# First convolution: the fourth row combination of every second unit moves from GpSimd to VectorE

## The reference

```python
x = x + _L0_conv_ref(_gn(x), ...)   # group norm, 1x1 conv to q, k, v, depthwise 3x3 conv,
                                    # attention over channels, 1x1 conv out
x = x + _L1_conv_ref(_gn(x))        # 3x3 patches, nearest channel per group, floor of products
```

```python
qkv = jax.lax.conv_general_dilated(x, w_qkv, (1, 1), 'SAME', dimension_numbers=DN) + b_qkv
qkv = jax.lax.conv_general_dilated(qkv, w_dw, (1, 1), 'SAME', dimension_numbers=DN, feature_group_count=3 * C) + b_dw
```

## Time and profile before

| what | us |
|---|---|
| median of 3 runs (lowest, highest) | 1471.12 (1470.74, 1479.9) |
| the profiled execution: its time | 1469.96 |
| its span in the profile | 1468.2 |
| first convolution, first image, about | 50 to 249 of the span |
| first convolution, second image, about | 768 to 967 of the span |

### The profile page before, as it was taken

One profiled execution on the slowest core, in us unless ns is written; L12 is line 12 of the kernel. 1 busy time (PEld: TensorE's weight loads), 2 busy tenths in 40 slices (PEclk: granted clock), 3 DMA queues, 4 the chain that ended last, 5 costly groups with the idle time before them and its releaser, 6 DMA issues. The chain is left out here.

```text
span 1468.2 us, 34011 instructions
## 1 busy us (share of the span) xinstructions
PE 1312.2 (89%) x13586; PEld 1050.8 (72%) x13586; DVE 1142.1 (78%) x1896; ACT 886.8 (60%) x1013; POOL 654.3 (45%) x672
## 2 busy tenths in 40 slices
PE   3889998996999599999979999989959968999998
PEld 1788897996899355555549998979949954555554
DVE  6577777477873699999967777745877838999998
ACT  3566664311553399999955556532135409999996
POOL 4888894242220244434038998814422113344400
PEclk9999999998999699999999999999979978999999
DMA  5466632593225344464427865319405235274533
GB/s 213 125 185 199 204 110 54 155 310 113 88 75 230 114 136 119 140 163 94 121 97 251 253 209 166 89 30 278 107 1 216 109 109 169 77 188 107 149 72 103
DMA packets 75876, 210.27 MB, mean 143 GB/s; under 512 B 15306, under 2 KB 15414, under 8 KB 72646
## 3 DMA queue, kind: packets, MB, share of 16 engines
q1 hardware_dynamic: 61214, 158.10, 34.1%
q0 software_dynamic: 6720, 36.93, 9.5%
q10 hardware_dynamic: 7784, 13.07, 3.3%
HBM read 91.54 MB, written 67.04 MB: 108 GB/s over the span
## 5 line engine op out<-in xcount | busy, mean ns | idle before, releaser
L1780 PE MATMUL acc<-rnd,ident 128*128 128x376 f32 x1152 | 391.9, 484 | 13.6 <-ACT rnd L1757 13.6
L1780 PEld LDWEIGHTS acc<-rnd,ident 128*128 128x128 f32 x1152 | 216.9, 192 | 134.0 <-ACT rnd L1757 15.0
L956 PE MATMUL ps_a<-wa,shared 128*128 128x192 f16 x1536 | 296.7, 247 | 9.3 <-DMA xc<-low 7.4
L956 PE MATMUL ps_a<-wb,xb 128*128 128x192 f16 x1536 | 295.5, 246 | 0.0
L1752 ACT ACTIVATE rnd_m<-prod,plus_round,scale 128x1504 f32<-128x1504 f32 x144 | 235.7, 1637 | 40.3 <-DVE prod L1603 30.3
L1716 DVE SCALAR_TENSOR_TENSOR over<-prod,scale,rnd 128x1504 bf16<-128x1504 f32 x144 | 256.4, 1783 | 0.0
L574 POOL TENSOR_TENSOR vt<-z 96x256 f32<-96x256 f32 x248 | 253.2, 1041 | 3.6 <-ACT z L850 3.5
L1757 ACT ACTIVATE rnd<-rnd_m,minus_round 128x1504 f32<-128x1504 f32 x144 | 223.2, 1550 | 4.7
L1660 POOL DMA_INDIRECT near<-f_planes,index x42 | 120.4, 2866 | 148.5 <-DVE prod L1603 142.4
L956 PEld LDWEIGHTS ps_a<-wa,shared 128*128 128x128 f16 x1536 | 150.6, 98 | 12.3 <-DMA xc<-low 8.5
L956 PE MATMUL ps_a<-wfa,shared 128*128 128x96 f16 x1536 | 155.7, 206 | 3.2 <-issue 2.8
(11 more groups left out here) (344 smaller groups left out, 2450.7 us busy)
## 6 DMA issues: line engine op xcount, KB each, us to landing
xb<-shared ACTq DMA_DIRECT2D x64, 195.0 KB, 2.7
f_planes<-img SPq DMA_DIRECT2D x8, 1536.0 KB, 14.1
shared<-f_planes SPq DMA_DIRECT2D x16, 768.0 KB, 5.8
v_a<-shared SPq DMA_DIRECT2D x40, 260.0 KB, 2.7
v_b<-xb SPq DMA_DIRECT2D x40, 260.0 KB, 3.1
shared<-v_a SPq DMA_DIRECT2D x40, 260.0 KB, 4.8
xb<-v_b SPq DMA_DIRECT2D x40, 260.0 KB, 5.5
v_c<-xc SPq DMA_DIRECT2D x40, 195.0 KB, 3.3
```

Source lines behind the costliest of these rows:

```text
L956: mm = lambda a, w, first, end: nc.tensor.matmul(out(i), a, w, start=first, stop=end)
L1780: nc.tensor.matmul(o(m), k["ident"][:, :], rnd[:, n % RNDS, BR * m:BR * m + BR, :], start=False, stop=False, skip_group_check=True)
```

## The change

In units 6, 8, ..., 30 (13 of 32, in each image) GpSimd leaves out combination 3; VectorE makes it, in `last_term`, at the end of its unit u-4 list, behind qk_low(2(u-4)+1). A semaphore `v_shared` counts these, and ScalarE's `high` and `norm` wait for it as well as for `v_made`.

```diff
+        SHARED = list(range(6, UNITS, 2))
+        shared_by = lambda u: sum(s <= u for s in SHARED)
...
                 for i, (p_, q_, op) in enumerate(V_TERMS):
-                    if i in which:
+                    if i in which and not (i == 3 and u in SHARED):
                         last = nc.gpsimd.tensor_tensor(out[:, i], row(p_), row(q_), op)
                 if 3 in which:
                     last.then_inc(v_made, 1)
...
+            def last_term(u):
+
+                at, out = 4 * (u % 4), vt[:, u % 2].rearrange("p (j i) x -> p i j x", i=4)
+                p_, q_, op = V_TERMS[3]
+                dve.wait_ge(normed, u + 2)
+                dve.wait_ge(lo_done, u - 1)
+                nc.vector.tensor_tensor(out[:, 3], z[:, at + p_:at + p_ + 3:2, :], z[:, at + q_:at + q_ + 3:2, :], op
+                                        ).then_inc(v_shared, 1)
...
                 qk_low(2 * u + 1)
+                if u + AHEAD + 1 in SHARED:
+                    last_term(u + AHEAD + 1)
...
                     act.wait_ge(v_made, u)
+                    act.wait_ge(v_shared, shared_by(u))
...
                     act.wait_ge(v_made, u - 3)
+                    act.wait_ge(v_shared, shared_by(u - 3))
```

More of the change, by code:

```diff
@@ L409 @@
             "outs", "o_s", "o_t", "o_a", "evac") \
-    + ("rows_ready0", "rows_ready1", "parts_in0", "parts_in1", "parts_in2", "saved0", "saved1", "saved2",
+    + ("v_shared", "rows_ready0", "rows_ready1", "parts_in0", "parts_in1", "parts_in2", "saved0", "saved1", "saved2",
        "dup_in0", "dup_in1", "dup_in2")
@@ L462, in attention @@
          att_pe, att_act, wf_split, pivot_in, pivot_out, outs, o_s, o_t, o_a, evac) = (sems[n] for n in ATT_SEMS[:34])
+        v_shared = sems["v_shared"]
+        SHARED = list(range(6, UNITS, 2))
+        shared_by = lambda u: sum(s <= u for s in SHARED)
         rows_ready = [sems[f"rows_ready{j}"] for j in range(2)]
```

## The result

The changed kernel took 1492.24 us (median of 4 runs, 1478.39 to 1498.25) against 1475.51 us (4 runs, 1470.74 to 1481.20) for the kernel before: a ratio of 1.0119, interval 1.0077 to 1.0161. The forecast was 1478.6 us with 1464 to 1485. The direction was right, the size was not: some 17 us lost instead of 7.5. The forecast started from 1471.1 us, the median of three runs of before; with the fourth run it is 1475.5, so 4.4 of the 13.6 us between 1478.6 and 1492.2 are the starting point.

What follows compares the result with a forecast made beforehand. The prediction took VectorE, ScalarE and GpSimd, not TensorE, to set the pace: 16 x 0.55 = 8.8, less 1.2, less 0.1, plus 7.5 us on 1471.1 gives 1478.6 us, range 1464 to 1485.

Steps and rivals of the forecast that it cites:

- the ring: VectorE, ScalarE and GpSimd waiting on one another in the first convolutions; said to set the pace, 6.11 or 6.21 us per unit.
- The turns: VectorE instructions with two SBUF inputs and GpSimd's never run together; when one ends, the other side's waiting instruction goes on.
- case A: At a changed boundary even_sum goes first after low; y_s at 4.32 us against a mean of 3.50, costing 0.82 us.
- case B: At a changed boundary VectorE keeps its turn behind low; y_s at 3.77 us against a mean of 3.50, costing 0.27 us.
- The second half: From y_s of a unit's first pair to y_s of its second; claimed to stay at 2.66 us.
- half A and half B: Equal mix of the two orders after low, because 24 of 55 kept the turn before: plus 0.55 us per plain boundary.
- plain boundaries: Second-pair y_s to next unit's first y_s, without transfer wait, small copies or cast: 16 places, 8.8 us lost.
- The second rival: Always even_sum first, also against last_term at the small copies: 13.1 plus 1.6, 14.7 us lost, 1485.8 us; beyond 1%: 0.07.
- the boundaries with ScalarE's small copies: First image, into units 5, 7, 11, 13, 15: GpSimd empty when low ends; gains 0.22 at four, 0.31 into 7, together 1.2 us.
- the cast: VectorE's 0.61 us instruction in the boundary into unit 3, first image: 4.32 or 3.77 against 4.13, about minus 0.1 us.
- the four places where a transfer was to hide the change: Into units 9 and 17 of each image, high waits 2.18 us for a transfer; last_term's 0.27 to 0.82 hides there, 0.
- The rival that rested on VectorE's twofold speed: VectorE keeps its turn over qk_low, last_term and td: y_s at 3.14, 7.1 us gained, 1464.0 us; chance 0.16.

Runs made afterwards that it cites:

- the first experiments: The changed kernel timed again unedited: 1488.37 us (6 runs), ratio 1.0131; the kernel before beside it took 1470.20 us (11 runs).
- in the gap: Against the changed kernel, same units: last_term moved between y_s and qk_low of the unit's first pair, where VectorE waits for ScalarE; 1462.01 us, ratio 0.9942.
- in all units and GpSimd held: last_term between the first pair's y_s and qk_low, units 4 to 30; GpSimd starts combinations 0 and 1 only after that pair's td; 1447.17 us, ratio 0.9834.

## Why the prediction was wrong

**Right.** The view that decided was the timeline of the ring, not the shares: GpSimd at 90% was relieved and the kernel became slower. The turns hold: the replay gave 4.32 for case A and 3.77 for case B, the traces show 4.31 to 4.33 and 3.78 to 3.79. The second half stayed at 2.66 us, and boundaries into even units stayed at 3.45 or 3.55, both with the few exceptions named under the table. TensorE's spare time of 0.35 us per unit was correctly taken as what is left above its 5.76.

**The step that failed** is "I take half A and half B, since before 24 of 55 kept the turn". The changed kernel took A at 15 of 16 plain boundaries. 16 x 0.55 = 8.8 us became 3.91 + 8.05 = 12.0. The share of the kernel before was no evidence for the kernel after: the change altered both lists at that point, and the outcome goes with the lists (1 of 19 with `last_term` behind `qk_low`, 15 of 19 without it). Why it does so stays open. The second rival ("always case A") was the right one at the plain boundaries (13.1 us forecast, 12.0 measured), and had too small a chance; its other half, a loss of 1.6 us at the small copies, did not come.

The sum was 9.2 us short of the 16.7 of the medians: 3.2 by this step, 1.9 by the smaller terms below, and some 4 by what the two traces do not show in the first convolutions at all.

**Terms that were a bit off.** At the boundaries with ScalarE's small copies I had `y_s` at 3.23. The timeline of after, into unit 13:

```profile
135.96 0.56 DVE L645 TENSOR_TENSOR y_s<-ps_a,td 128x384 f32<-128x384 f32 x1 [0.54 <-POOL td L585]
...
138.10 0.41 DVE L632 TENSOR_TENSOR vt<-z 96x256 f32<-96x256 f32 x1
138.24 0.99 POOL L585 TENSOR_TENSOR td<-side 128x192 f32<-128x192 f32 x1 [1.69 <-ACT side L884]
138.43 0.35 DVE L638 TENSOR_TENSOR td<-side 128x192 f32<-128x192 f32 x1
139.32 0.56 DVE L645 TENSOR_TENSOR y_s<-ps_a,td 128x384 f32<-128x384 f32 x1 [0.54 <-DVE td L638]
```

GpSimd was empty when `low` ended, as I wrote, but then `td` too went ahead of `even_sum`, which ended at 3.27, and `y_s` needs both: 3.36 us, a gain of 0.09 and not 0.22. Into unit 5 it was 3.25 and into 7 3.93, with 3.83 forecast. Together 0.66 us and not 1.2. At the cast I took nearly nothing and it cost 0.32 (4.45 for 4.13). And of the four places where a transfer was to hide the change, the two in the second image showed 0.72 us: into unit 9 the boundary and second half went from 6.95 to 7.19, into 17 from 6.79 to 7.27.

**From 12.6 to 17 us.** The trace's own sum is 3.69 + 8.91 = 12.6 us, its Gram copies say 13.5; 1.7 us more arose between the two first convolutions. The span grew by only 8.6 us, so some 5 us came back behind the second Gram copy. Instruction by instruction, ScalarE is 13.5 us late at that copy, 10.9 some 140 us later, and 8.4 at its end. The 140 us behind the copy, before and then after:

```profile
969.00:1109.00 140.00, 120.91 (x2270) 113.81 (x2268) 94.65 (x320) 40.48 (x73) 43.65 (x78) 0.93 0.40 107
```

```profile
982.50:1119.90 137.40, 118.93 (x2269) 112.31 (x2268) 94.66 (x320) 40.47 (x73) 43.69 (x78) 0.94 0.39 109
```

The same work took 2.6 us less there, at a granted clock of 0.93 and 0.94 of full speed (2.4 GHz). Another 2.2 us came back over the last 255 us, at 0.99 in both. So the clock can hold a part of it at most, and where the rest came from is open.

The medians went the other way. In the runs of the first experiments the mean granted clock over the span was 0.9609 before (11 runs) and 0.9567 after (6). Seven runs of before at 0.962 or more took 1468.9 us in the mean, the two of after at 0.963 1479.8: 10.9 more. The two of before at 0.957 or less took 1474.6 us, the four of after there 1491.4. A straight line of time against clock, through 35 of the 36 runs of before (without one of 1487.05) and through all ten of the changed kernel, gives 1470.9 and 1485.0 us at a clock of 0.960: 14.1 us apart, give or take some 3. So I estimate that a part of the 17 us, some 3 to 4, goes with a lower mean clock of TensorE in the changed kernel's runs. Whether the change lowers it or the runs fell so is open: there are too few runs for that, and no kernel here changes the clock alone.

**Moving work between the two engines.** The Trainium skill (Perfetto Trace Analysis, section Optimizing Scalar/DVE Operations) says that moving operations between GpSimd and VectorE might not help, since they share a port. The measured ratios agree with "might": 1.0131 with `last_term` behind `qk_low`, 0.9942 with it in the gap, 0.9834 with it there in all units and GpSimd held. The rival that rested on VectorE's twofold speed (0.41 against 0.72 us) did not come about in the place where the change put the instruction.

## What to carry to other kernels

When two engines take turns at a shared resource, the price of a moved instruction is not its duration: it is its own turn, and one of the other engine's turns for each gap it opens there, filled with whatever that engine has pending next. Look what stands behind the removed instruction in its engine's list before a gain is counted, and put the added one where its engine waits anyway: 0.41 us of VectorE cost 0.86 us behind `qk_low` and 0.03 in the gap. All this holds when the other engine has something pending; where it had nothing, the added instruction cost only itself (3.78 us into unit 27). A share of outcomes counted in the kernel before (24 of 55) is no chance for the kernel after, if the change touches the list at that point; both outcomes belong in the range.

## What the runs showed that I had not expected

Behind VectorE's `low`, with `qk_low` and an instruction of GpSimd both waiting, the kernel before went either way (24 to 31), and GpSimd's way at all 49 boundaries without constants once two fulfilled waits stood behind `qk_low` in VectorE's list. An instruction that is not even due yet, or a wait that costs no time of its own, goes with who gets the turn; that it is the cause is not shown. And the same program's runs differ by 15 us (1481.19 to 1495.90) in step with TensorE's mean granted clock, 0.963 to 0.952, which is as much as the whole effect looked for: runs of unlike clock should not be set against each other one by one.
